# A fused adapter matmul and hyper-connection block on one core: y written by ScalarE ahead of an adding load

## What is computed

```python
def _L0_cond_ref(x, weight, adapter_ids):          # x (8, 512, 2048), weight (8, 2048, 2048)
    w = weight[adapter_ids]
    return jnp.einsum('bsi,boi->bso', x, w)
...
def _L0_ffn_ref(x, W_res, W_pre, W_post, H_res_base, H_pre_base, H_post_base, gate, W_branch):
    ...
    # n = 4 streams of C = 512 columns; sinkhorn_log does 50 steps
    x_norm = x * jax.lax.rsqrt(jnp.mean(x * x, axis=-1, keepdims=True) + RMS_EPS)
    H_res_logits = (x_norm @ W_res.T).reshape(B, T, n, n) + H_res_base
    H_pre_logits = x_norm @ W_pre.T + H_pre_base
    H_post_logits = x_norm @ W_post.T + H_post_base
    H_res = sinkhorn_log(H_res_logits)
    H_pre = jax.nn.softmax(H_pre_logits, axis=-1)
    H_post = jax.nn.softmax(H_post_logits, axis=-1)
    g = jax.nn.sigmoid(gate)[0]
    H_res = (1.0 - g) * I + g * H_res
    x_streams = x.reshape(B, T, n, C)
    x_pre = jnp.einsum('btnc,btn->btc', x_streams, H_pre)
    y = x_pre @ W_branch
    x_mixed = jnp.einsum('btij,btjc->btic', H_res, x_streams)
    y_distributed = jnp.einsum('btc,btn->btnc', y, H_post)
    return (x_mixed + y_distributed).reshape(B, T, nC)
x = x + _L0_ffn_ref(_L0_cond_ref(x, L0_cond_weight, itok_B_3_7), ...)
```

## Time and profile before

| | before |
|---|---|
| time, median of 3 runs | 1854.85 us |
| the profiled execution's own time | 1854.1 us |
| its span | 1852.0 us |
| mean granted TensorE clock | 0.968 |
| TensorE, VectorE, ScalarE, GpSimd busy | 92%, 85%, 35%, 3% |
| busy share of the DMA engines' time, queue of SP | 38.2% |
| core memory traffic | 202.58 MB read, 33.55 MB written |

### The profile page before, as it was taken

The page is one execution under the profiler, slowest core; times in us unless marked ns, Lnnn a source line. Parts: engine busy times, 40 slices in busy tenths (PEclk is TensorE's granted clock), DMA queues, the critical chain, the costliest instruction groups (busy, mean ns, idle before and its releaser), DMA issues.

```text
span 1852.0 us, 24465 instructions
## 1 busy us (share of the span) xinstructions
PE 1698.9 (92%) x7690; PEld 1366.3 (74%) x7690; DVE 1578.4 (85%) x6128; ACT 648.4 (35%) x1031; POOL 47.2 (3%) x40
## 2 busy tenths in 40 slices
PE   9999999989999999899999989999999999999704
PEld 7888887777877788787877778777887778777601
DVE  4323599996999889996999969998799978999899
ACT  4334433333233433234333433234332343332503
POOL 0000000000000000000000000000000000000404
PEclk9999999999999999999999999999999999999857
DMA  6224323453335523263234532355233633336002
GB/s 232 91 90 140 123 92 114 151 196 109 97 110 193 181 92 126 92 229 123 92 122 135 198 125 92 114 175 193 87 117 100 227 129 99 116 117 216 9 1 91
DMA packets 65073, 237.72 MB, mean 128 GB/s; under 512 B 7344, under 2 KB 7472, under 8 KB 64816
## 3 DMA queue, kind: packets, MB, share of 16 engines
q1 hardware_dynamic: 64944, 236.17, 38.2%
HBM read 202.58 MB, written 33.55 MB: 128 GB/s over the span
## 4 chain that ended last, share of the span: by engine, by line
DVE 65%; PE 28%; issue 2%; DMA 2%; ACT 2%; SPq 1%; DVEq 0%; ACTq 0%
PE acc L976 25%; DVE piece L851 16%; DVE w_lo L612 10%; DVE work L788 9%; DVE vec L786 8%; DVE vec L784 8%; DVE xpre L817 3%; DVE cond_t L650 3%; DVE x_lo L620 2%; DVE x_raw L877 2%; DMA w_raw<-wt 1%; DVE xpre_t L828 1%; SPq L218 1%; DMA out<-piece 1%; DVE xpre L815 1%
## 5 line engine op out<-in xcount | busy, mean ns | idle before, releaser
L976 PE MATMUL acc<-w_hi,x_hi 128*128 128x512 f32 x2048 | 817.2, 399 | 2.1 <-DVE w_lo L612 2.1
L976 PE MATMUL acc<-w_hi,x_lo 128*128 128x512 f32 x2048 | 803.9, 393 | 0.0
L976 PE MATMUL acc<-w_lo,x_hi 128*128 128x512 f32 x2048 | 803.0, 392 | 0.0
L976 PEld LDWEIGHTS acc<-w_hi,x_hi 128*128 128x128 f32 x2048 | 388.8, 190 | 83.8 <-DVE w_lo L612 2.4
L976 PEld LDWEIGHTS acc<-w_hi,x_lo 128*128 128x128 f32 x2048 | 387.7, 189 | 83.7
L976 PEld LDWEIGHTS acc<-w_lo,x_hi 128*128 128x128 f32 x2048 | 388.7, 190 | 78.0
L612 DVE TENSOR_TENSOR w_lo<-w_raw,w_hi 128x1024 fp32r<-128x1024 f32 x256 | 312.2, 1222 | 157.1 <-ACT w_hi L382 153.7
L382 ACT ACTIVATE w_hi<-w_raw 128x1024 fp32r<-128x1024 f32 x256 | 270.0, 1057 | 450.8 <-DMA w_raw<-wt 450.6
L851 DVE SCALAR_TENSOR_TENSOR piece<-cond,kern,piece 128x512 f32<-128x512 f32 x448 | 301.5, 745 | 0.0
L788 DVE TENSOR_TENSOR work<-kern,vec 128x32 f32<-128x32 f32 x1536 | 251.1, 202 | 0.0
L786 DVE RECIPROCAL vec<-vec 128x8 f32<-128x8 f32 x1536 | 242.3, 199 | 0.1
(11 more groups left out here) (109 smaller groups left out, 747.8 us busy)
## 6 DMA issues: line engine op xcount, KB each, us to landing
w_raw<-wt SPq DMA_DIRECT2D x256, 512.0 KB, 3.5
x_raw<-xt SPq DMA_DIRECT2D x64, 512.0 KB, 4.5
piece<-xn SPq DMA_DIRECT2D x56, 512.0 KB, 4.4
out<-piece SPq DMA_DIRECT2D x56, 512.0 KB, 3.4
x_raw<-xn SPq DMA_DIRECT2D x8, 512.0 KB, 4.6
out<-x_raw SPq DMA_DIRECT2D x8, 512.0 KB, 2.7
cond<-wb SPq DMA_DIRECT2D x1, 1024.0 KB, 14.6
cond<-wall SPq DMA_DIRECT2D x1, 192.0 KB, 12.6
```

What stands on the lines that cost most here:

```text
L976: mm = nc.tensor.matmul(acc[t][:], stationary, moving, start=(chunk == 0 and m == 0), stop=(chunk == CHUNKS - 1 and m == 2))
```

## The change

ScalarE now writes a piece first: `spread_y` waits for the tile's y and for the slot's earlier store, and writes y times the post weight of each of the two streams (`SPREAD_AT`). GpSimd then issues a load that adds x onto the piece (`accum_op`), and signals `residual_in`, for which `mix` waits as before. `mix` has four terms per stream. SP's loads of x into the pieces are gone. `turn_pre` waits for `y_spread` instead of `mixed`. `pre`, the turn, the split and the branch of tiles 2 and 3 are at earlier units.

```diff
--- before.py
+++ after.py
@@ -73,14 +73,14 @@
 BLOCK_AT = (3, 12)
 FAST_AT = ((5, 12), (13, 20))
 FINAL_AT = 20
-PRE_AT = (8, 12, 16, 24)
-PRE_T_AT = (10, 14, 23, 26)
-PRE_SPLIT_AT = (11, 15, 24, 27)
-Y_AT = (13, 17, 25, 28)
+PRE_AT = (8, 12, 16, 20)
+PRE_T_AT = (10, 14, 18, 22)
+PRE_SPLIT_AT = (11, 15, 19, 23)
+Y_AT = (13, 17, 20, 24)
 MIX_AT = (21, 22, 24, 25, 26, 27, 29, 30)
-RESIDUAL_AT = (14, 15, 16, 17, 24, 25, 26, 27)
+SPREAD_AT = (14, 14, 18, 18, 25, 25, 27, 28)
 STORE_AT = (23, 24, 26, 27, 28, 29, 31, 31)
-DVE_STEPS = 404 + BLOCKS * FAST * 6
+DVE_STEPS = 388 + BLOCKS * FAST * 6
 ASKS, DONES = 9, 10
 
 
@@ -182,6 +182,7 @@
         summed, summed_copied = sem("summed"), sem("summed_copied")
         step = sem("step")
         mixed = sem("mixed")
+        y_spread = sem("y_spread")
         residual_in = [sem(f"residual_in{i}") for i in range(OUT_SLOTS)]
         stored = [sem(f"stored{i}") for i in range(OUT_SLOTS)]
 
@@ -295,19 +296,12 @@
                         if unit >= UNITS:
                             load_weights(following, b, unit)
                     for q in range(MIX_PAIRS):
-                        slot, use = q % OUT_SLOTS, q // OUT_SLOTS
+                        slot = q % OUT_SLOTS
                         if end and U == STORE_AT[q]:
                             place = index((b - 1) * MIX_PAIRS + q)
                             sp.wait_ge(mixed, 1 + (b - 1) * MIX_PAIRS + q + 1)
                             sp.dma_start(rows(out, place), piece[:, slot, :, :]
                                          ).then_inc(stored[slot], 16)
-                        if end and U == RESIDUAL_AT[q]:
-                            place = index((b - 1) * MIX_PAIRS + q)
-                            if use > 0:
-
-                                sp.wait_ge(stored[slot], ((b - 1) * 2 + 1) * 16)
-                            sp.dma_start(piece[:, slot, :, :], rows(xn, place)
-                                         ).then_inc(residual_in[slot], 16)
                     if not last and U > 3 * PASS_UNITS:
                         load_x(b + 1, U - 3 * PASS_UNITS - 1,
                                pieces_of=b if end and U == UNITS - 1 else None)
@@ -325,6 +319,18 @@
             nc.gpsimd.affine_select(out=ident[:], in_=ident[:], compare_op=ALU.not_equal,
                                     fill=1.0, base=0, pattern=[[-1, P]],
                                     channel_multiplier=1).then_inc(ident_ready, 1)
+
+            def add_residual(c, q):
+
+                place, slot = c * MIX_PAIRS + q, q % OUT_SLOTS
+                pool.wait_ge(y_spread, (place + 1) * 2)
+                nc.gpsimd.dma_start(piece[:, slot, :, :], xn[bass.ds(place, 1), :, :]
+                                    .rearrange("a p (s c) -> (a p) s c", s=2),
+                                    accum_op=ALU.add).then_inc(residual_in[slot], 16)
+
+            for c in range(BATCHES - 1):
+                for q in range(MIX_PAIRS):
+                    add_residual(c, q)
 
             def ending():
                 first_tile = (BATCHES - 1) * TILES
@@ -545,6 +551,16 @@
                 answer(ask, work[:], work[:], ACT.Exp)
                 answer(ask + 1, vec[:, LOG, :], vec[:, SUM, :], ACT.Ln)
                 answer(ask + 2, work[:], work[:], ACT.Exp)
+
+            def spread_y(c, q):
+
+                slot, (t, p) = q % OUT_SLOTS, divmod(q, 2)
+                act.wait_ge(y_ready, c * TILES + t + 1)
+                act.wait_ge(stored[slot], (c * MIX_PAIRS + q) // OUT_SLOTS * 16)
+                for s in range(2):
+                    nc.scalar.activation(piece[:, slot, s, :], y_ps[t % 2][:], ACT.Copy,
+                                         scale=logit[:, t, NRES + STREAMS + 2 * p + s:][:, 0:1]
+                                         ).then_inc(y_spread, 1)
 
             def body(b, parity, end):
                 last = isinstance(b, int) and b == BATCHES - 1
@@ -597,6 +613,9 @@
                                 act.wait_ge(y_ready, (b - 1) * TILES + t)
                             nc.scalar.activation(xpre_t[:, 0, :], y_ps[t % 2][:], ACT.Copy
                                                  ).then_inc(pre_hi_ready, 1)
+                    for q in range(MIX_PAIRS):
+                        if end and U == SPREAD_AT[q]:
+                            spread_y(b - 1, q)
                     if u == PASS_UNITS - 1:
                         for t in range(TILES - 1):
                             evacuate(b, parity, n, t)
@@ -835,23 +854,17 @@
                     slot = q % OUT_SLOTS
                     dve.wait_ge(residual_in[slot], (c * 2 + q // OUT_SLOTS + 1) * 16)
                     written = [0, 0]
-                    for j in range(STREAMS + 1):
+                    for j in range(STREAMS):
                         for s in range(2):
                             i = 2 * p + s
-                            if j < STREAMS:
-                                source = cond[:, 1 - parity, j, t, :]
-                                weight = kern[:, t * NRES + i * STREAMS + j:][:, 0:1]
-                            else:
-                                source = y_ps[t % 2][:]
-                                weight = logit[:, t, NRES + STREAMS + i:][:, 0:1]
-                                if s == 0:
-                                    dve.wait_ge(y_ready, c * TILES + t + 1)
+                            source = cond[:, 1 - parity, j, t, :]
+                            weight = kern[:, t * NRES + i * STREAMS + j:][:, 0:1]
                             if j > 0:
                                 after(written[s])
                             ins = nc.vector.scalar_tensor_tensor(
                                 out=piece[:, slot, s, :], in0=source, scalar=weight,
                                 in1=piece[:, slot, s, :], op0=ALU.mult, op1=ALU.add)
-                            if j == STREAMS and s == 1:
+                            if j == STREAMS - 1 and s == 1:
                                 ins.then_inc(mixed, 1)
                             else:
                                 written[s] = mark(ins)
@@ -1017,7 +1030,7 @@
                 tile = c * TILES + t
                 pe.wait_ge(pre_ready, tile + 1)
 
-                pe.wait_ge(mixed, 1 + c * MIX_PAIRS + max(0, t - 1) * 2)
+                pe.wait_ge(y_spread, (c * TILES + max(0, t - 1)) * STREAMS)
                 for k in range(C // P):
                     cols = slice(k * P, (k + 1) * P)
                     mm = nc.tensor.transpose(y_ps[t % 2][:, cols], xpre[:, cols], ident[:])
```

## The result

The changed kernel takes 1802.51 us (median of 4 runs, 1800.78 to 1805.26) against 1854.06 us (4 runs) of the kernel before on the same chip: a ratio of 0.9722, with a 95% interval of 0.9706 to 0.9739. That is 2.8% faster, inside the range of the prediction and 14.5 us above its forecast of 1788 us.

The account below looks back on a forecast made before the run. TensorE bounds the kernel, held up only where VectorE is late. 1854.1 us less 52.9 of waits and 14 of clock is 1787.2, plus 0.75 for the median: 1788 us, 3.6% faster; range 1779 to 1817.

Parts of the forecast that it names:

- GpSimd was not starved: Rival, chance 0.06: load descriptors get written only while VectorE stands still, so mixing waits for slow loads; 1895 us.
- The rule of the Trainium skill: GpSimd, writing its loads' descriptors, is shut out during VectorE's two-port mode: load an estimated 22 us, time about 1850 us.
- the rival in which pieces wait for the load: Rival, chance 0.03: VectorE's freed time goes into waiting for an adding load landing after some 23 us; 1851 to 1858 us.
- The wait of the bank: Before tile 2's turn_pre, after unit 23: 20.1 us go through its new release, with some 6.5 us of clock loss.
- So 1.93 us go per piece, 15.4 us per batch.: VectorE's mixing: dropping the last two of ten terms per piece saves 1.93 us, 15.4 us per batch.
- With 15.4 us less VectorE is through its last piece at 831.9.: Batch's end: VectorE's last piece ends at 831.9 instead of 847.3, so unit 0's 20.1 us of waits go.
- That was the source of the waits like 861.36 (5.7 us), which go too.: TensorE soon after unit 0: SP, held at the last two stores, loaded weights late; these 5.7 us of waits vanish.
- The first rival: Batch's end stays late through ScalarE or SP; unit 0 keeps 20.1 + 7.5 us, 1815 us; chance 0.12.
- The adding load: GpSimd's load of x onto pieces: 7 us, between bounds 4.4 and 14.6; at 7 us nothing waits.
- ScalarE's added work: Sixteen activations of 0.598 us per batch, 9.6 us, cost nothing, hidden in ScalarE's waiting for weights; its store wait is free.
- Units 18, 20 and 28: TensorE's waits: unit 18's 12.5 us stay, half of unit 20's (2.9 us) and unit 28's 4.1 us go.
- The clock: TensorE's nine half-clock stretches last 29.88 us; some 14 us are lost there and were counted as gone.

Follow-up runs that it names:

- run 2: Kernel after with one term per stream repeated, so VectorE's work is that of the kernel before: 1854.28 us, ratio 0.9999.
- Run 1: Kernel before with the y term left out of every piece, loads, banks and units unchanged: 1794.86 us, ratio 0.9688.
- run 3: Kernel after with a plain load in place of the adding one, y missing in the output: 1790.81 us, ratio 0.9664.
- Runs 4 and 5: Kernel after: one without SP's wait for all stores, 1783.43 us; the other with SP reading the adapter number once, 1788.74 us.
- run 6: Kernel after without SP's wait for all stores and with a plain load in place of the adding one: 1781.08 us, ratio 0.9598.
- Run 4: Kernel after without SP's wait for all stores before the next batch's loads: 1783.43 us, ratio 0.9623.

## Why the prediction was right or wrong

By its own steps:

- *What bounds the kernel, and the rivals.* Right. TensorE waits for a late VectorE, and run 2 shows it from the other side: with VectorE's work restored nothing is gained. GpSimd was not starved: the adding load landed within 5.2 to 10.9 us, and the plain load from the same queue took the 4.5 us of a load from SP, beside mixing without a gap. The rule of the Trainium skill ("SBUF — State Buffer", the bandwidth-pool intuition), by which the prediction had estimated 1850 us, was not seen at work here (as the prediction says, the terms beside these loads are of the slower form, so this is no test of it), nor was the rival in which pieces wait for the load.
- *The wait of the bank.* It went, as said (20.1 us). But the prediction named the new release as the cause. Run 1 shows that two shorter pieces ahead of it do the same, 1.4 us left.
- *"So 1.93 us go per piece, 15.4 us per batch."* This term failed: it was 1.31 us and 10.5 us. The prediction added the chain's 0.52 us of "issue" to the 1.41 us of the last two terms, as if VectorE stood there. The timeline counts from start to start. VectorE in the kernel before:

```profile
771.43 5.39 DVE L851 SCALAR_TENSOR_TENSOR piece<-cond,kern,piece 128x512 f32<-128x512 f32 x8
776.74 1.41 DVE L851 SCALAR_TENSOR_TENSOR piece<-y_ps,logit,piece 128x512 f32<-128x512 f32 x2
778.05 1.22 DVE L612 TENSOR_TENSOR w_lo<-w_raw,w_hi 128x1024 fp32r<-128x1024 f32 x1
```

And in the kernel after:

```profile
551.83 5.38 DVE L864 SCALAR_TENSOR_TENSOR piece<-cond,kern,piece 128x512 f32<-128x512 f32 x8
557.13 1.22 DVE L631 TENSOR_TENSOR w_lo<-w_raw,w_hi 128x1024 fp32r<-128x1024 f32 x1
```

Eight terms take 5.31 us to the start of what follows before (771.43 to 776.74) and 5.30 us after (551.83 to 557.13). The 0.52 us were the time of the eighth term, which the chain had put under another name. The two y terms took 778.05 - 776.74 = 1.31 us. The window's 10.4 us less per batch agree, and so do the page's 72.6 us over 56 pieces, 1.30 each.
- *"With 15.4 us less VectorE is through its last piece at 831.9."* This came 7.4 us too early in effect: 8 x 0.62 = 4.9 us from the term above, and some 2.5 us where `x_lo` waits ahead of the seventh piece. VectorE in the kernel after:

```profile
601.68 1.23 DVE L639 TENSOR_TENSOR x_lo<-x_raw,x_hi 128x1024 fp32r<-128x1024 f32 x1 [2.48 <-ACT x_hi L395]
```

The waits of unit 0 went all the same (0.95 of 20.1 us left), since the forecast had 11 us of room there.
- *"That was the source of the waits like 861.36 (5.7 us), which go too."* Here most of the miss comes out: 13.1 us stand there instead of none. The source was rightly named, and SP's chain behind the last mix kept its length of 14 us. Counted from the wait in unit 18, that mix ends 8.0 us earlier (847.35 - 749.36 = 98.0 before, 616.40 - 526.38 = 90.0 after; eight pairs of terms are 10.5, less the 2.5 of `x_lo`). But TensorE, with its other waits gone, is ready for the projection 9.6 us earlier (861.36 - 0.84 - 749.36 = 111.2, and 630.43 - 2.49 - 526.38 = 101.6). So its wait there grew by 1.6 us, from 0.84 to 2.49. With the forecast's 15.4 us it would have gone, as it says; with 10.5 us it would be at about nothing in this batch (0.84 + 9.6 - 10.5), and the late `x_lo` makes the rest. Two terms failed here, then: the relief, taken at 15.4 for 10.5 us, and the adding load, costed at nothing. Run 1, with the 10.5 us and no adding load, has 6.5 us at this place, and run 3, with the plain load, 5.1: about half of the 13.1 us belongs to each. No term of the sum followed SP beyond the store, so the sum didn't show how little room there was. The first rival named SP's wait for the stores, but put it in unit 0, one projection too early, and at 20 + 7.5 us. Runs 4 and 5 shorten two different links of the chain, and each gives back 13 to 18 us with the clock's part, about the forecast's whole error of 14.5 us.
- *The adding load.* The price was right (7 us taken, 6.8 measured), and "at 7 us nothing waits" is true of the pieces. That it is therefore free is not: run 3 puts the addition at 8 to 11 us, through later loads of x. With SP's store wait gone (run 6) it is some 5 us or less.
- *ScalarE's added work.* The price of 0.598 us was right. The record of each of the 112 activations lasts 0.689 us, but they overlap: 68.5 us of busy time are 0.61 each. The work hides as said; the waits for stores are free.
- *Units 18, 20 and 28.* 12.5 us stayed in unit 18, 2.3 us in unit 20 (2.9 forecast), unit 28's 4.1 us went. All right.
- *The clock.* 13.2 us less busy time against 14 in the sum, and that is partly luck. The sum counted the nine stretches at 29.88 us, from the first L976 of each on, and left out the matmuls ahead of it. Run 4, which has no half-clock stretch here, is busy 1680.1 us with the same 7690 matmuls, 18.8 us less than before: that is what the nine cost, not 14. Three are left, worth 5.6 us, two of them behind the new late projections.
- *Sum.* The forecast missed 52.9 - 39.8 = 13.1 us of idle time and 0.8 us of clock. The 14.1 us at the start of the next batch, less 0.6 us won in unit 20, are 13.5: the first miss is this one wait, up to 0.4 us.

**Still open:** how the addition delays the loads of x, and so what a schedule without that delay would give. Their median hardly moves (5.6 against 5.4 us), only some of them are late (the slowest took 10.6 us against 8.8), and no run separated a busier queue from slower transfers. That the whole of run 3's gain passes through `x_lo` is argued from the place and size of its 8.9 us, not shown by a run of its own.

## What to carry to other kernels

Price an instruction of a dependent row by its distance from start to start in the timeline; a piece of "issue" in a chain can be the end of the instruction before it. When a change removes an engine's lateness, follow every in-order queue that feeds the same place to its end: here SP's wait for a store, a number read from memory and a weight load were a chain of constant length, hidden as long as TensorE was held elsewhere. And a transfer that nobody waits for is not yet free: look at what its neighbours wait for.

## What the runs showed of the hardware

- A load that adds onto SBUF (512 KB, from GpSimd's queue) took a median of 6.8 us from issue to landing, where a plain one from the same queue took 4.5 and one from SP 4.4. GpSimd spends 0.86 us on each issue.
- ScalarE's copy out of PSUM lasts 0.598 us by its record for 128x512 (`cond<-acc`), and 0.689 us when it is scaled by a value per partition (`piece<-y_ps,logit`). In a row the latter overlap: four of them take 2.42 us (from 360.09), and 112 keep ScalarE busy for 68.5 us.
- The same on VectorE: a term of a piece lasts 0.744 us by its record, and eight dependent ones take 5.30 us, 0.66 each.
- SP needs 3.0 us to read a number from memory and work out the address from it (619.49 to 622.50), and issues nothing else of its queue meanwhile.
- In the kernel after the granted clock fell to 0.5 (1.2 GHz) behind waits of TensorE of 2.77 and 3.20 us at projections, and not behind those of 1.20 to 2.49 us at the same place. It also fell once, at 943.3 us, behind a wait of only 1.84 us. In run 1 it did not fall behind one of 2.71 us (1042.64) but did behind one of 1.86 us (938.05), so length alone doesn't decide it.
